# A third buffer for the copied weights in the first layer's loop over sorted expert tiles

## The reference

```python
gout = xt @ Wg.T                      # router, 8 experts
topv, topi = jax.lax.top_k(gout, 2)
w = jax.nn.softmax(topv, axis=-1)
comb = einsum('tke,tk->te', one_hot(topi, 8), w)
g = einsum('th,efh->etf', xt, W1) + b1[:, None, :]     # 128 -> 256
v = einsum('th,efh->etf', xt, W2) + b2[:, None, :]
h = silu(g) * v
eo = einsum('etf,ehf->eth', h, W3) + b3[:, None, :]    # 256 -> 128
out = einsum('eth,te->th', eo, comb)
```

## Time and profile before

| | us |
|---|---|
| median of 3 runs | 1304.48 |
| lowest and highest | 1303.97, 1309.03 |
| the profiled execution's own time | 1310.25 |
| its span, first to last instruction | 1308.5 |
| the loop's first and last up matmuls | 243.2, 310.9 |

### The profile page before, as it was taken

One profiled execution on the slowest core, in us unless ns is written; L12 is line 12 of the kernel. 1 busy time (PEld: TensorE's weight loads), 2 busy tenths in 40 slices (PEclk: granted clock), 3 DMA queues, 4 the chain that ended last, 5 costly groups with the idle time before them and its releaser, 6 DMA issues. The chain is left out here.

```text
span 1308.5 us, 29552 instructions
## 1 busy us (share of the span) xinstructions
PE 1096.4 (84%) x9991; PEld 808.5 (62%) x9999; DVE 800.7 (61%) x2758; ACT 546.6 (42%) x1207; POOL 378.3 (29%) x515
## 2 busy tenths in 40 slices
PE   8999887784998884799977768886788989899892
PEld 4666655674466851556645325553776979889792
DVE  5566255344588868645677874556953757757424
ACT  4366642474544322222223122323123746648483
POOL 2344406343100620000000115540034434524442
PEclk9899988998998566799998877998978999999997
DMA  1210449222000059079743255544902212032222
GB/s 46 51 41 4 145 160 372 63 64 77 1 2 3 5 190 336 1 160 184 288 172 137 86 180 132 141 97 155 297 13 72 66 35 67 21 71 46 56 53 66
DMA packets 112948, 135.94 MB, mean 104 GB/s; under 512 B 16948, under 2 KB 78471, under 8 KB 112145
## 3 DMA queue, kind: packets, MB, share of 16 engines
q1 hardware_dynamic: 100208, 119.26, 30.1%
q0 software_dynamic: 12592, 14.79, 4.5%
HBM read 67.92 MB, written 69.32 MB: 105 GB/s over the span
## 5 line engine op out<-in xcount | busy, mean ns | idle before, releaser
L2204 PE MATMUL m_psY<-large,m_hT 128*128 (+2 forms) x992 | 139.2, 284 | 0.0
L2204 PEld LDWEIGHTS m_psY<-large,m_hT 128*128 128x128 f32 x992 | 126.7, 191 | 0.1
L2124 POOL DMA_INDIRECT rows<-m_ys,m_slot x93 | 90.7, 975 | 116.5 <-DVE m_slot L2360 107.1
L626 DVE TENSOR_REDUCE at_peaks<-at_ps 128x3 f32<-128x384 f32 x128 | 65.4, 551 | 45.9 <-PE at_ps L389 45.9
L538 ACT ACTIVATE at_PT<-at_ps,at_bias 128x384 f32<-128x384 f32 x128 | 67.3, 577 | 48.0 <-PE at_ps L399 47.9
L2260 ACT ACTIVATE m_hT<-m_psH 128x512 f32<-128x512 f32 x124 | 73.7, 594 | 30.1 <-PE m_psH L2186 29.7
L331 POOL TENSOR_SCALAR_AFFINE_SELECT at_PT<-at_PT 128x256 f32<-128x256 f32 x128 | 54.8, 430 | 72.0 <-ACT at_PT L538 68.1
L1515 POOL IOTA row_no<- 128x1 f32 x1 | 0.1, 132 | 251.2 <-SPq L744 251.2
L2186 PE MATMUL m_psH<-m_xT,large 128*128 128x128 f32 x512 | 67.6, 275 | 0.0
L2272 ACT ACTIVATE m_ys<-m_psY,m_weight 128x144 f32<-128x144 f32 x124 | 47.3, 381 | 42.8 <-PE m_psY L2204 38.2
L2186 PE MATMUL m_psH<-m_xT,m_up 128*128 128x128 f32 x480 | 63.6, 276 | 0.0
(11 more groups left out here) (738 smaller groups left out, 2806.0 us busy)
## 6 DMA issues: line engine op xcount, KB each, us to landing
rows<-blank SPq DMA_DIRECT2D x16, 2448.0 KB, 21.3
m_xs<-rows SPq DMA_DIRECT2D x124, 76.5 KB, 2.0
pair_rows<-blank SPq DMA_DIRECT2D x1, 8320.0 KB, 26.1
large<-in_L_attn_firs SPq DMA_DIRECT2D x4, 2048.0 KB, 18.9
large<-comb_rows SPq DMA_DIRECT2D x64, 128.0 KB, 5.8
se_wu<-in_L_ffn_up SPq DMA_DIRECT2D x32, 192.0 KB, 2.6
W2T<-in_L_ffn_down_turned SPq DMA_DIRECT2D x1, 4096.0 KB, 12.5
large<-in_L_ffn_up SPq DMA_DIRECT2D x4, 1024.0 KB, 8.6
```

Of the source, the lines that this page charges most:

```text
L626: nc.vector.tensor_reduce(peaks[:, b % 2, n, :], psS[:, u % TILES, 0:CAUSAL].rearrange("p (x c) -> p x c", c=P), AX.X, ALU.max).then_inc(r ...
L2124: pool.indirect_dma_start(k.rows[(layer + 1) % 2], bass.IndirectOffsetOnAxis(slot[:, q:q + 1], 0), ys[:, q, :], None, bounds_check=E3 * N ...
L2204: m = nc.tensor.matmul(psY[b][:, 0:wide], hT[b][:, c * P:(c + 1) * P], w, start=(c == 0), stop=(c == C - 1))
```

## The change

`up` gets three buffers, and tile j uses buffer j modulo 3 in all four places where it is written or read. The copy into it, which waited for the matmuls and the hidden product of the tile two back, now waits for those of the tile three back, and the third copy doesn't wait for them at all. The order of the instructions in each queue is the same.

```diff
+    UPS = 3
...
-        xT, up, sg, hT = ([sb(f"{n}{i}", [P, w]) for i in range(2)]
-                          for n, w in (("xT", P), ("up", WIDE0), ("sg", F0), ("hT", F0)))
+        xT, sg, hT = ([sb(f"{n}{i}", [P, w]) for i in range(2)] for n, w in (("xT", P), ("sg", F0), ("hT", F0)))
+        up = [sb(f"up{i}", [P, WIDE0]) for i in range(UPS)]
...
-                        m = nc.tensor.matmul(psH[b][:, c * P:(c + 1) * P], up[b][:, c * P:(c + 1) * P], xT[b][:],
+                        m = nc.tensor.matmul(psH[b][:, c * P:(c + 1) * P], up[j % UPS][:, c * P:(c + 1) * P], xT[b][:],
...
-                    if j >= 2:
-                        act.wait_ge(*up_done.at(j - 1))
-                        act.wait_ge(*hid_done.at(j - 1))
-                    nc.scalar.activation(up[b][:], W[:, bass.ds(e, WIDE0)], ACT.Copy).then_inc(picked.sem, 1)
+                    if j >= UPS:
+                        act.wait_ge(*up_done.at(j - UPS + 1))
+                        act.wait_ge(*hid_done.at(j - UPS + 1))
+                    nc.scalar.activation(up[j % UPS][:], W[:, bass.ds(e, WIDE0)], ACT.Copy).then_inc(picked.sem, 1)
...
-                                                 bias=up[b][:, 2 * F0 + c:2 * F0 + c + 1])
+                                                 bias=up[j % UPS][:, 2 * F0 + c:2 * F0 + c + 1])
...
-                            scalar=up[b][:, 2 * F0 + C + c:2 * F0 + C + c + 1], in1=sg[b][:, c * P:(c + 1) * P],
+                            scalar=up[j % UPS][:, 2 * F0 + C + c:2 * F0 + C + c + 1], in1=sg[b][:, c * P:(c + 1) * P],
```

## The result

| | us |
|---|---|
| before, beside it: median of 4 runs (lowest, highest) | 1306.76 (1303.97, 1313.12) |
| after: median of 4 runs (lowest, highest) | 1292.32 (1289.5, 1293.9) |
| ratio, 95% interval | 0.9895 [0.9866, 0.9924] |
| the profiled execution of after: time, span, clock | 1289.5, 1287.8, 0.888 |
| loop, first to last up matmuls, before and after | 66.86, 50.41 |

The kernel is faster by 14.4 us (16.1 was forecast), and the place is right. On two other chips, where the kernel before is slower too, the same kernel gained 0.2% (not clear of nothing) and 0.4%; that came out in the experiments and is the part that the forecast didn't have. Lines of after stand one higher than before: L1152 is the weight copy, L1106 the up matmuls, L1117 the down projection.

What follows compares the result with a forecast made beforehand. The prediction took a ring of waits through the hidden product, 1.96 us a tile, as the bound. 32 tiles at 1.48 save 15.4 us, the start 0.8: 1304.5 - 16.1 = 1288.4 us, range 1285.0 to 1294.5.

Steps and rivals of the forecast that it cites:

- The ring through the hidden product: First layer's tile loop: copy, silu, hidden product, copy two tiles on set 1.95 us a tile; three buffers make it 0.98.
- TensorE next, at 0.11 + 0.89 + 0.45: Same loop after the change: transpose to up, up to down, down to next transpose bound a tile at 1.45 us.
- The taken 1.48: Forecast period of the loop: TensorE's 1.45 us plus a little for ScalarE close behind; 32 tiles save 15.4 us.
- ScalarE's term: ScalarE's need per tile in the loop, copy to silu to output copy to next copy: 1.43 to 1.55 us.
- rival A: ScalarE becomes the loop's bound, period over 1.51 us; at 1.55 the gain is 13.9 us; chance 0.20.
- The start, 0.77: Start of the loop: the third tile's up matmuls begin at 246.60 instead of 247.37, 0.77 us earlier.
- The end, nothing: From the last up matmuls to the last scatter: nothing gained or lost beyond 0.1 us.
- From the profiled execution to the median: The whole kernel's 16.1 us gain, found on the profiled execution, is taken equally off the median: 1304.5 to 1288.4.
- the forecast alone: Whole kernel, with the loop's period at 1.45 to 1.51 us: gain 15.2 to 17.1 us; chance 0.68.
- Rival C: Denser matmuls in the loop get the 1.2 GHz clock; wholly there it costs 24.5 us, 1329; chance 0.04.
- break-even: Share of the loop's time at 1.2 GHz at which the loop would be even: 39% (0.51 / 1.3).
- Rival B: Another wait in the loop replaces the removed one, period above 1.78 us, time within 0.5%; chance 0.08.

Runs made afterwards that it cites:

- e2: Changed kernel with three buffers, but the weight copy waits for the tile two back as in the kernel before; ratio to before 1.001, loop 66.04 us.
- e4: Kernel before, two buffers, with biases read from the resident array through a register, so the copy doesn't wait for the hidden product; ratio to before 0.9953.
- i1: Changed kernel with plain writes of 128 consecutive rows instead of the indirect scatter, on a slower chip; loop 49.41 us in one run.
- j1: Changed kernel without edit, on a chip of the faster kind; 1286.8 us against 1301.94 before, ratio 0.9864, loop 50.60 us.
- h1: Changed kernel without edit, measured again on a chip of the slower kind; ratio to before 0.9961, loop 66.21 us.
- h2: Changed kernel with one down matmul per tile instead of two, on a slower chip; ratio to before 0.9998, loop 64.26 us.
- h3: Changed kernel with the output copy moved from ScalarE to VectorE, on a slower chip; 1314.29 us against 1325.02 before, ratio 0.9904.
- e1: Changed kernel without edit, in more rounds on a slower chip; 1324.71 us against 1325.6 before, ratio 0.9981, loop 57.96 us.

## Why the prediction was right, and where it was not

- **The ring through the hidden product**: right. e2 brings the 1.96 back by the waits alone, e4 removes most of the wait (1.55) by taking the hidden product out of it.
- **TensorE next, at 0.11 + 0.89 + 0.45**: right to the hundredth. The taken 1.48 was 0.03 too much between tiles without disturbance; but two pairs of 1.62 and 1.52 stand in every trace of the dense loop on kind A and in i1, at the same tiles (10 to 12 and 23 to 25, counted from 0), so the third to the last set took 47.13 us (j1: 46.90), a mean of 1.47. 62.71 - 47.13 = 15.6, for 15.4 forecast. In after's pairs the copy is late by "issue"; why wasn't tried.
- **ScalarE's term mis-sized**: output copy to weight copy was taken as 0.40 to 0.52. That 0.40 is no floor: where ScalarE is behind, the distance is 0.25 (19 of 31 times in h1, 26 of 31 in h2), so ScalarE needs 1.29 and rival A had little ground; h3 bears it out. The row of the fourth layer showed an instruction behind one that had waited. The Trainium skill (ScalarE: Activation LUTs, What ACT_TABLE_LOAD costs) has some 93 ns of overlap between back-to-back ACTIVATEs; the runs agree after all, with 0.37 - 0.25 = 0.12 and 0.63 - 0.54 = 0.09. It changed nothing, since TensorE was the later one.
- **The start, 0.77**: over-sized, by the clock. The prediction took the second set of up matmuls at 1.48, as before, on the ground that nothing ahead of it changes. Stretches from one set to the next, one of before, then two of after:

```profile
243.22:245.16 1.94, 1.94 (x10) 1.94 (x10) 0.35 (x2) 0.00 (x0) 0.00 (x0) 0.50 0.36 93
...
244.90:246.25 1.35, 1.35 (x10) 1.35 (x10) 0.35 (x2) 0.00 (x0) 0.00 (x0) 0.73 0.25 64
246.25:248.18 1.93, 1.93 (x11) 1.93 (x10) 0.96 (x4) 1.15 (x3) 0.00 (x0) 0.50 0.29 71
```

  The granted clock, down after TensorE had waited for the first rows, is up again 2.8 us behind the first set in before, 4.0 in after and 3.5 in j1. So the second set took 1.92 in after and 1.79 in j1 for 1.48, and the third stood behind it: second to third set went from 2.21 to 1.93 in after (0.28) and to 1.73 in j1 (0.48), and not by 0.77. In after the first interval was shorter besides (1.94 to 1.35), since it began before the clock fell; the change doesn't touch that, so it is luck that first to third set came out at 0.87 (4.15 to 3.28). In j1 it was 0.45 (3.70).
- **The end, nothing**: right, 5.46 both times. In the loop as a whole 16.45 (j1: 16.26) for 16.1.
- **From the profiled execution to the median**: 16.1 off 1306.76, before's median in the same comparison, would be 1290.7; measured 1292.32. That lies above what the forecast alone gave (1287.4 to 1289.3) and inside the whole range, 1285.0 to 1294.5; 2.3 of it is that before's median rose from 1304.48 to 1306.76 with its fourth run.
- **Rival C, the clock**: didn't come in the loop; 1.00 in the middle. Its break-even is misnamed: 0.51 / 1.3 = 39% is a share of the tiles, not of the time.
- **Rival B, another wait within half a per cent**: not on kind A, but on kind B this is what happens (0.9981, 0.9961), by a thing that was none of its candidates: neither a late scatter slot nor the matmuls. The profile of before was taken on one chip and couldn't show it: at 1.96 its loop has no stall, nor has e2's on kind B, and the fourth layer's last loop stalls on kind B only.

Left open: what about the indirect scatter delays TensorE's signals (or its work) on kind B, and whether it is the chip or a state of it; why the loop took 58 us in e1 and 66 us in h1 with the same kernel, while the medians put h1 ahead (0.9961, 0.9981); whether another order of scatters avoids it.

## What to carry to other kernels

A wait for several semaphores is read from the timeline with the step numbers in hand, not from the releaser column; then every ring that is left is summed, and the largest is the forecast. A distance behind an instruction that waited is no floor for an engine: look for the same pair where the engine is behind. What stands at a loop's start may take another time in the next execution, if the clock changes there. A gain of about a per cent that comes of packing an engine densely is to be timed on several chips, since what else runs beside it (here GpSimd's indirect DMAs) may cost on some of them only.

## What was not expected of the hardware

Chips differ by some 20 us on the same kernel (medians of 1302 to 1307, and 1320 to 1327). On the slower ones, indirect scatters by GpSimd beside dense matmuls come with stalls in which TensorE's signals act some 1.5 to 1.8 us late (1.80 from transpose to copy in h1 and 2.09 in h2, 263.83 to 265.92, for 0.31), three tiles in 6.1 us in h1. With two passes fewer the pace under stalls is nearly the same (1.89 us a tile for 1.95), and a plain write of the same bytes has none. The stalls come at the same two tiles of the fourth layer's last loop in all nine traces of these chips, and in none of the five of the others.
